# A new order of scores, values and projection on TensorE in a cross-attention and mixture-of-experts kernel, and GpSimd in place of VectorE for six small biases

## What is computed

```python
x = x + xattn(layernorm(x), ctx, Wq, bq, Wkv, bkv, Wp, bp)   # x: 2 x 512 x 512, ctx: 2 x 1024 x 512
x = x + ffn(layernorm(x), Wg, Wu, Wd, Wr, temperature)       # 8 experts, 512 x 512 each

def xattn(...):                    # 16 heads of 32, all 1024 query rows against all 2048 context rows
    q, k = fq_sym(q, per row), fq_sym(k, per row)            # rounded to -127..127 times a step
    v = fq_sym(v, per column)
    attn = fq_unsigned(softmax(q @ k.T), per row)            # rounded to 0..255 times a step
    return (attn @ v) @ Wp + bp
```

## Time and profile before

| | us |
|---|---|
| median of three runs | 721.15 |
| lowest and highest run | 719.05, 723.45 |
| profiled execution | 722.4 |
| its span, first to last instruction | 720.6 |
| attention tiles 1 to 7, in that span | 160.5 to 432.0 |

### The profile page before, as it was taken

The page is one execution under the profiler, slowest core; times in us unless marked ns, Lnnn a source line. Parts: engine busy times, 40 slices in busy tenths (PEclk is TensorE's granted clock), DMA queues, the critical chain, the costliest instruction groups (busy, mean ns, idle before and its releaser), DMA issues.

```text
span 720.6 us, 16044 instructions
## 1 busy us (share of the span) xinstructions
PE 617.9 (86%) x5440; PEld 334.1 (46%) x5440; DVE 567.7 (79%) x930; ACT 460.4 (64%) x560; POOL 409.7 (57%) x457
## 2 busy tenths in 40 slices
PE   8999998666777777777768787799999999999995
PEld 4744443333534343343435355455555555555543
DVE  6998888999999999999999998793746547464430
ACT  5444459789888899898989896443534434343421
POOL 5265576655677878787877773324334453344503
PEclk9999999999999999999999997999999999999998
DMA  7877879999999999999999996258796887968724
GB/s 261 203 152 174 183 155 189 170 173 175 182 174 182 181 198 189 192 193 186 195 189 186 192 188 151 88 197 230 180 251 140 225 218 182 251 151 230 140 33 59
DMA packets 318517, 129.44 MB, mean 180 GB/s; under 512 B 293508, under 2 KB 293508, under 8 KB 318472
## 3 DMA queue, kind: packets, MB, share of 16 engines
q1 hardware_dynamic: 311296, 112.64, 72.7%
q0 software_dynamic: 7168, 16.26, 10.8%
q10 hardware_dynamic: 8, 0.01, 0.0%
HBM read 44.33 MB, written 12.06 MB: 78 GB/s over the span
## 4 chain that ended last, share of the span: by engine, by line
PE 49%; issue 11%; DMA 11%; DVE 11%; SPq 8%; ACT 5%; POOL 3%; POOLq 0%; DVEq 0%; ACTq 0%
PE psum L1724 46%; DMA work<-work 9%; DVE spare L1452 4%; ACT work L1104 4%; SPq L485 3%; SPq L483 3%; DVE spare L1443 3%; POOL work L676 1%; PE psum L1901 1%; SPq L452 1%; PE psum L2052 1%; DMA token_region<-in_L_xattn_Wkv_dram 1%; PE psum L1729 1%; POOL out_dram L858 1%; DMA work<-x_rows,slot_tok 0%
## 5 line engine op out<-in xcount | busy, mean ns | idle before, releaser
L1104 ACT ACTIVATE work<-spare,exp_bias 128x2048 uint8<-128x2048 f32 (+1 forms) x127 | 253.2, 1994 | 32.7 <-POOL exp_bias L682 21.4
L1452 DVE TENSOR_SCALAR_CACHE_REDUCE spare<-psum,q_step_now 128x1024 f32<-128x1024 f32 x128 | 162.3, 1272 | 3.4 <-PE psum L1901 3.2
L676 POOL CAST work<-work 128x2048 int16<-128x2048 uint8 x70 | 132.4, 1892 | 33.9 <-DMA work<-work 25.5
L1443 DVE TENSOR_SCALAR_CACHE_REDUCE spare<-psum,q_step_now 128x2048 f32<-128x2048 f32 x64 | 150.2, 2347 | 1.7 <-PE psum L1901 1.6
L1901 PE MATMUL psum<-keys_region,work 128*128 128x512 f16 x256 | 74.4, 395 | 42.5 <-DVE spare L1452 23.1
L846 POOL DMA_INDIRECT work<-x_rows,slot_tok x32 | 52.1, 1627 | 86.1 <-DVE slot_w L1656 72.7
L1901 PE MATMUL psum<-keys_region,bias_hl 128*128 128x512 f16 x256 | 71.0, 383 | 30.3 <-DVE spare L1452 22.9
L858 POOL DMA_INDIRECT out_dram<-keys_region,slot_tok x32 | 51.7, 1616 | 73.1 <-ACT keys_region L1199 66.1
L1860 PEld LDWEIGHTS psum<-values_region,work 128*128 128x128 f16 x2016 | 65.8, 96 | 32.1 <-POOL work L676 19.3
L1724 PE MATMUL psum<-work,spare 128*128 128x480 f16 (+1 forms) x396 | 79.4, 360 | 0.4 <-DVE work L1629 0.4
L1724 PE MATMUL psum<-work,keys_region 128*128 128x480 f16 x384 | 78.9, 366 | 0.0
(11 more groups left out here) (250 smaller groups left out, 1009.0 us busy)
## 6 DMA issues: line engine op xcount, KB each, us to landing
spare<-in_L_ffn_Wd_dram SPq DMA_DIRECT2D x8, 1024.0 KB, 15.3
spare<-in_L_ffn_Wg_dram SPq DMA_DIRECT2D x7, 1024.0 KB
spare<-in_L_ffn_Wu_dram SPq DMA_DIRECT2D x7, 1024.0 KB, 11.0
work<-in_ctx_dram SPq DMA_DIRECT2D x3, 1024.0 KB, 5.8
work<-work SPq DMA_TRANSPOSE x174, 3.7
token_region<-in_L_xattn_Wkv_dram SPq DMA_DIRECT2D x2, 1024.0 KB, 6.1
resid<-in_x_dram SPq DMA_DIRECT2D x2, 1024.0 KB, 8.8
out_dram<-work SPq DMA_DIRECT2D x8, 256.0 KB, 2.6
```

The costliest lines, as they stand in the source:

```text
L676: nc.gpsimd.tensor_copy(p_T_int[h % 4], pair_bytes[h % 4]).then_inc(unpacked, 1)
L1104: nc.scalar.activation(p_out, scores, ACT.Exp, bias=exp_bias[:, h % 4:h % 4 + 1], scale=-1.0, accum_out=p_sum[:, h:h + 1]).then_inc(exp_do ...
L1443: nc.vector.tensor_scalar(stage_home(h, first), psum[:, at:at + 4, :].rearrange("p b k -> p (b k)"), q_step_now[:, h:h + 1], None, ALU.mul ...
L1452: nc.vector.tensor_scalar(stage_home(h, first)[:, 1024 * c:1024 * c + 1024], psum[:, at:at + 2, :].rearrange("p b k -> p (b k)"), q_step_n ...
```

## The change

On TensorE, the pair's order becomes: first half of `h + 1`; in the pair of head 12 projection pieces 2 and 3; values of `h - 6`; two throwaway matmuls, left out in the pairs of head 10 and 12 after tile 0; second half of `h + 1`; first half of `h + 2`; values of `h - 5`; second half of `h + 2`; in the pair of head 10 projection pieces 0 and 1. On GpSimd, tile 0's biases of the heads 5, 7, 9, 11, 13 and 15 are made in its own queue, and VectorE no longer makes them; ScalarE's waits are counted anew for it.

```diff
@@ GpSimd, tile 0
             pool.wait_ge(vT_in[1], 32)
+            make_bias(0, 5)
             unpack(0, 2, True)
+            make_bias(0, 7)
             unpack(0, 4)
...
             for h in (6, 8, 10):
+                make_bias(0, h + 3)
                 unpack(0, h)
+            make_bias(0, H - 1)
             attention_half(0, 0, True)
             unpack(0, 12)
@@ VectorE
-                    if first and h > 2:
+                    if first and h == 4:
                         make_bias(i, h - 1)
-                    if after_first and h == 0:
-                        make_bias(0, H - 1)
@@ TensorE, in the loop over even h
                     scores(i, h + 1, 0, first)
...
-                    for head in (h - 6, h - 5):
-                        if head >= 0:
-                            values(i, head, not first)
-                        elif not first:
-                            values(i - 1, head + H, True)
-                        if head % 2 == 0 and (h or not first):
-                            throwaway(6 + head % H // HQ if head >= 0 or not first else 6, 2 if head >= 0 or not first else 8)
-                    if not first:
-                        after_attention(i - 1, h)
+                    if h == 12 and not first:
+                        project_parts(i - 1, (2, 3))
+                    values_at(i, h - 6, first)
+                    if (h or not first) and (first or h not in (10, 12)):
+                        throwaway(6 + (h + H - 6) % H // HQ if h >= 6 or not first else 6, 2 if h >= 6 or not first else 8)
                     scores(i, h + 1, 1, first)
...
                     if h < H - 2:
-                        for n in range(2):
-                            scores(i, h + 2, n, first)
+                        scores(i, h + 2, 0, first)
+                    values_at(i, h - 5, first)
+                    if h < H - 2:
+                        scores(i, h + 2, 1, first)
+                    if h == 10 and not first:
+                        project_parts(i - 1, (0, 1))
```

More of the change, by code:

```diff
@@ L46 @@
 PV_RANK = (1, 2, 3, 4)
-PROJECT_AT = (10, 10, 12, 12)
 BYTE_HEADS = (0, 2, 4, 6, 8, 9, 10, 12, 14)
@@ L1082, in attention_tile @@
                         act.wait_ge(v_halved, ROUNDED.index(h) + 1)
-                    if first:
+                    if first and h < 5:
                         act.wait_ge(edge_bias, h + 1)
                     elif h % 2 and (following or not after_rows or h < H - 1):
-                        act.wait_ge(bias_made, HQ * i - HQ + h // 2 + 1)
+                        act.wait_ge(bias_made, HQ * i + h // 2 - 1)
                     else:
-                        act.wait_ge(edge_bias, H + HQ * i - HQ + (h + 1) // 2 + 1)
+                        act.wait_ge(edge_bias, HQ * i + (h + 1) // 2 + 3)
                     if not following and h == H - 1:
@@ L1463, in make_bias, with attention_tile @@
                     nc.vector.tensor_scalar(exp_bias[:, at], s_low[:, at], LN255, None, ALU.add).then_inc(edge_bias, 1)
-            def attention_tile(i, first, after_first=False):
+            def attention_tile(i, first):
                 for h in range(0, H, 2):
@@ L1490, in _ @@
             attention_tile(0, True)
-            attention_tile(1, False, after_first=True)
+            attention_tile(1, False)
             with dve.Fori(2, QT - 1) as i:
@@ L1871, in project, with project_parts @@
                                pieces=pieces, start=0 in pieces, stop=DK - 1 in pieces)
[L1873 to L1882, removed]
+            def project_parts(j, parts):
+                for n in parts:
+                    columns = slice(n * P, n * P + P)
+                    if n == 0:
+                        pe.wait_ge(wp_ready, DK)
+                    ins = project(bank(7)[:, columns], j, columns)
+                    if n == DK - 1:
+                        ins.then_inc(proj_full, 1)
             def scores(i, h, n, first):
@@ L1908, in throwaway, with values_at @@
                     nc.tensor.matmul(bank(b)[:, 256:512], key_parts[:, 0, 0:P], key_parts[:, 0, 0:256], start=True, stop=True)
+            def values_at(i, head, first):
+                if head >= 0:
+                    values(i, head, not first)
+                elif not first:
+                    values(i - 1, head + H, True)
             def attention_tile(i, first):
```

## The result

The change made the kernel a little slower: a median of 725.63 us (721.24 to 739.99, 20 runs) against 720.71 us of the kernel before in the same comparison (717.93 to 723.99, 20 runs), a ratio of 1.0064 with a 95% interval of 1.0043 to 1.0085. The profiled execution took 725.22 us, its span 723.5. Forecast were 718.4 us and a range of 714.9 to 722.4.

What follows compares the result with a forecast made beforehand. The prediction took a GpSimd, ScalarE and DMA loop to bound the middle tiles, slightly longer than VectorE's circuit. Gains of 0.7 + 2.4 = 3.1 us, taken as 2.7 on the 721.15 median, gave 718.4 us, range 714.9 to 722.4.

Steps and rivals of the forecast that it cites:

- The throwaways and the clock: TensorE: dropping two pairs' throwaway matmuls costs 0; the standstill before tile 6's half clock comes no more often than before.
- The odd values product: TensorE: second half waits for one values product, not two; VectorE can gain up to 3.2 us if nothing else holds it.
- The projection: TensorE, pairs of heads 10 and 12: moved pieces just fit, cost 0, at worst 0.2 us a tile, 1.4 in all.
- The loop: Middle tiles: GpSimd, ScalarE and DMA circuit of 38.42 to 39.04 us, waiting for neither VectorE nor TensorE, outlasts VectorE's 38.05.
- The signs: Tiles 2 to 7: VectorE's waits for scores nearly gone, replaced by exponential waits; head 9's unpack every 38.4 us in 3 to 6.
- Rival 1: Tiles 1 to 7: VectorE is the bound after all, every tile falls to 38.05 us, total 715.3 us; chance 0.14.
- Tile 0's biases: Tile 0: six biases leave VectorE at 0.12 us each, a gain of 0.7 us, bounds 0 to 0.7.
- The end: After tile 7: statistics start 1.2 us earlier, a step avoids GpSimd's unpack, ScalarE normalises at 435.4, not 437.79: 2.4 us gained.
- Rival 3: Tiles 2 to 7: head 15's late values product delays the attention half, 0.7 us a tile, total 724.7 us; chance 0.09.
- The sum: Whole kernel: 0.7 + 2.4 = 3.1 us off the profiled 722.4; with half the 1.25 offset, 2.7 off the median.

Runs made afterwards that it cites:

- values_moved: The kernel before with only the odd head's values product moved behind the next head's first half; 726.09 us, ratio 1.007.
- projection_moved: The kernel before with only the projection pieces moved, throwaway matmuls kept in all pairs; 721.5 us, ratio 1.0.
- order_only: The kernel before with TensorE's part of the diff alone; 727.61 us, ratio 1.0096.
- fill10_pair10: The changed kernel with ten throwaway matmuls instead of two, and also in the pair of head 10; 720.19 us, ratio 1.0.
- fill6: The changed kernel with six throwaway matmuls instead of two where it has any; 724.65 us, ratio 1.0057.
- biases_only: The kernel before with GpSimd's six biases of tile 0 alone; 719.33 us, ratio 0.9989.

## Why the prediction was wrong, point by point

- **The throwaways and the clock: the step that failed.** It read: "That standstill is what the new order removes, so I expect it not more often than before", at cost 0. The runs showed 4.9 us more instead of the 2.7 less of the forecast. One fall had been read, together with the one wait in front of it. What went with the clock is the idle pieces of every pair, and those the move of the odd values product made longer: 1.08 us in values_moved, 1.16 in the change, where projection_moved has 0.66. Falls went from 2 to 6 (8 in values_moved, 11 in order_only), and time at half clock in tiles 1 to 7 from 3.8 to 20.5 us. The Trainium skill (TensorE: Matmul & The Clock Gate, A second HAM failure mode: psum-queue depth-cycling) describes this: short idling between groups of matmuls that cycle through PSUM banks lets the clock go up and down. The traces here agree, with scores written to six banks in turn and idle pieces of 1.05 to 1.16 us between them, and the forecast had not weighed it.
- **The odd values product.** "VectorE can gain up to its 3.2 us" is not seen in any time. Where the clock keeps up, tiles of VectorE last 38.14 us, near the 38.05 of the forecast, but in no trace more than two in a row. The move was costed only by when scores are ready, not by what gap it used to fill.
- **The projection.** Right for the change, with the clock at 1.00: it "fits by almost nothing", and the pair of head 12 lasts 4.87 us where 4.81 is usual, within the 0 to 0.2 us a tile. With ten throwaways ahead of it, in fill10_pair10, it no longer fits (5.10).
- **The loop.** Right in size: 38.3 to 38.7 us from unpack to unpack in tiles 3 to 5, where nothing outside held GpSimd, and 26.89 to head 7's bias. The 0.6 us more of tile 6 was counted as uncertain and stands in every trace. The effect, that the loop holds VectorE, is argued and not shown. And "nothing in it waits for VectorE" holds only while VectorE is on time: behind two falls it was late by 0.81 and 1.07 us, and the stretch was 28.70. So a loss off the loop got onto it.
- **The signs.** "Waits for ScalarE's exponentials stand in their place" came in no version: no trace has VectorE waiting for ScalarE in tiles 1 to 7. If the loop held VectorE, it was by way of GpSimd's unpacks and TensorE's queue behind them.
- **Rival 1 (VectorE is the bound after all).** Not borne out: no version came near 715.3 us, and fill10_pair10, with no fall in its trace, took 720.19. It is not refuted either. VectorE is as good as always busy in the tiles of 38.14 us, and in fill10_pair10, whose tiles last 38.6, TensorE's scores still hold it up by 0.5 us a tile. Against it speaks that three tiles of fill6 add up to the loop's pace.
- **Tile 0's biases, 0.7 us.** Pairs of tile 0 now take 4.74 us, as forecast:

```profile
135.59 2.35 DVE L1446 TENSOR_SCALAR_CACHE_REDUCE spare<-psum,q_step_now 128x2048 f32<-128x2048 f32 x1
...
140.33 2.35 DVE L1446 TENSOR_SCALAR_CACHE_REDUCE spare<-psum,q_step_now 128x2048 f32<-128x2048 f32 x1
```

  and tile 1 starts 1.2 us earlier, in biases_only 0.7; but in fill10_pair10, with the same biases, it starts 0.4 us later than before, so one execution can't tell the term. The 0.7 are 0.1%, and the interval of biases_only reaches from -0.4% to +0.2%: the runs allow it and can't confirm it.
- **The end, 2.4 us.** Wrong even without falls. In fill10_pair10 the statistics started at 431.87, as forecast (431.9), but a step was held again, by an unpack that had come earlier too. VectorE:

```profile
433.88 1.85 DVE L1504 SCALAR_TENSOR_TENSOR ln_rstd<-ln_b,ln_rstd 128x1 f32<-128x1 f32 x1
```

  GpSimd's unpack of head 12 in that kernel:

```profile
433.82 1.89 POOL L675 CAST work<-work 128x2048 int16<-128x2048 uint8 x1 [0.50 <-DMA work<-work]
```

  and ScalarE, tile 6's rows normalised:

```profile
436.60 0.81 ACT L1059 ACTIVATE work<-work,row_shift,ln_rstd 128x512 f32<-128x512 f32 x1 [1.85 <-DVE row_shift L1556]
```

  ScalarE normalised at 436.60 and not at 435.4: 1.2 us of the 2.4 were there. I had moved VectorE and left the unpack where it stood, though it hangs on the DMA queue (its wait was 1.31 us in the earlier trace rows, 0.50 here) and came 1.46 us earlier.
- **Rival 3 (slower by the attention half).** Its sign came true and its mechanism did not: in the change ScalarE waited once for a values product, in tile 1, where the fall at 171 made that product late too. In values_moved it waited four times, 0.3 to 1.5 us, so there the mechanism may have a share that no run separates.

```profile
173.58 0.39 ACT L1043 ACTIVATE work<-psum 128x256 f32<-128x256 f32 x1 [1.34 <-PE psum L1861]
```

- **The sum.** Half of the 1.25 us of offset gives a gain of some 2.5 us, not 2.7; the 0.3 us decide nothing.

The chances of a slower kernel stood on one mechanism only. A rival "the clock falls in more pairs", for which the idle pieces of the earlier trace rows and the 0.96 of tile 6 in the earlier trace rows spoke, was missing.

## What to carry to other kernels

When TensorE isn't the bound and its clock is seen to fall, moving work between its gaps is an edit of the clock too: list the idle pieces of a cycle before and after, not only their sum, and see whether the work that is moved was filling the longest. A loop over several engines can be looked for by a stretch that repeats to 0.02 us while waits around it vary; but check how much lateness of the engines outside it turns them into a part of it. A list of waits can leave out the short ones: here four of them made 0.5 us a tile, and only the length of the pairs showed them. When one thing is moved out of another's way, ask whether the other moves too.

## What the runs showed of the hardware

Useless matmuls sped a kernel up: ten of 128x256 in 1.25 us, eight pairs a tile but one, raised TensorE's busy time from 26.6 to 33.0 us in a tile without a fall and took the time from 0.64% above the kernel before to level with it. And 69 us of idling in 88 pieces went with eight falls, in 138 pieces with one. What exactly the clock looks at, these runs don't say.
